# Moving the convolution norms of the last eight token tiles out of the attention-only stage

## The reference

```python
# convolution y from an FFT of the S4D taps, then:
r = x + (y + x * D)
out = (r - mean(r)) * rsqrt(var(r) + 1e-5) * ln_w + ln_b     # norm 0
x = layernorm(x + out)                                       # norm 1
x = layernorm(x + cross_attention(x, ctx))                   # norm 2
x = layernorm(x + mlp(x) + experts(x))                       # norm 3
# experts: top-8 of 64 keys on each of two sides, 4 heads; top-8 of the 64 sums;
# softmax over them; silu(x . down[idx]) * weight, times up[idx], summed
```

## Time and profile before

| | us |
|---|---|
| median of 3 runs | 667.06 |
| lowest, highest | 664.38, 668.99 |
| the profiled execution, its own time | 664.58 |
| its span | 662.8 |

### The profile page before, as it was taken

How to read it: one execution, slowest core, us unless ns; L and a number is a source line. 1 busy time by engine, 2 the same in 40 slices (tenths; PEclk the granted TensorE clock), 3 DMA queues, 4 the chain that set the end, 5 groups by cost and what they waited for, 6 DMA issues and landing times.

```text
span 662.8 us, 9603 instructions
## 1 busy us (share of the span) xinstructions
PE 580.7 (88%) x3132; PEld 376.8 (57%) x3132; DVE 491.4 (74%) x966; ACT 397.5 (60%) x554; POOL 310.4 (47%) x346
## 2 busy tenths in 40 slices
PE   5568688937695989999999999998999999998996
PEld 2246465726363644547775654776655588443585
DVE  7997966483468868978568797857779795778782
ACT  4776463311432659976548786673878773777760
POOL 0747576592524474433536342364632352753451
PEclk9679999977957689999999999999999999999999
DMA  8591325684610000000000000000000000000000
GB/s 233 195 389 41 104 74 154 165 209 28 257 60 0 2 0 0 1 0 1 1 0 17 8 10 1 0 1 0 17 9 8 0 1 1 17 8 8 0 15 18
DMA packets 19851, 34.13 MB, mean 51 GB/s; under 512 B 7265, under 2 KB 14178, under 8 KB 18338
## 3 DMA queue, kind: packets, MB, share of 16 engines
q1 hardware_dynamic: 15425, 29.32, 14.4%
q10 hardware_dynamic: 4376, 4.20, 2.1%
HBM read 21.81 MB, written 10.52 MB: 49 GB/s over the span
## 4 chain that ended last, share of the span: by engine, by line
PE 68%; DVE 13%; ACT 9%; issue 5%; POOL 3%; DMA 2%; POOLq 0%; DVEq 0%; ACTq 0%; SPq 0%
PE banks L820 22%; PE banks L910 8%; PE banks L915 8%; PE banks L865 5%; PE banks L887 3%; PE banks L842 3%; PE banks L877 3%; PE banks L708 3%; PE banks L698 2%; PE banks L735 2%; PE banks L851 2%; ACT arena L931 2%; DVE stats L1460 2%; PE banks L902 2%; DVE arena L1548 1%
## 5 line engine op out<-in xcount | busy, mean ns | idle before, releaser
L1256 POOL TENSOR_TENSOR arena<-arena 128x1024 f32<-128x1024 f32 x64 | 126.3, 1973 | 156.2 <-ACT arena L1129 155.1
L820 PE MATMUL banks<-arena 128*128 128x512 f32 x384 | 174.2, 596 | 6.0 <-issue 3.9
L820 PEld LDWEIGHTS banks<-arena 128*128 128x128 f32 x384 | 69.9, 190 | 83.4 <-issue 77.5
L1129 ACT ACTIVATE arena<-arena 128x1024 f32<-128x1024 f32 x64 | 73.5, 1149 | 7.5 <-DVE arena L1546 3.2
L1131 ACT ACTIVATE arena<-arena 128x1024 f32<-128x1024 f32 x64 | 73.5, 1149 | 2.1
L1548 DVE SCALAR_TENSOR_TENSOR arena<-arena 128x1024 f32<-128x1024 f32 x48 | 65.1, 1357 | 1.7
L1227 POOL TENSOR_SCALAR arena<-mv 128x1 f32<-128x1 f32 (+1 forms) x40 | 14.4, 360 | 104.0 <-DVE mv L1461 102.6
L1019 ACT COPY arena<-banks 128x512 f32<-128x512 f32 (+1 forms) x64 | 34.1, 532 | 46.8 <-PE banks L812 31.2
L910 PE MATMUL banks<-arena 128*128 128x256 f32 x256 | 58.4, 381 | 2.7 <-DVE arena L1570 1.3
L915 PE MATMUL banks<-arena 128*128 128x256 f32 x256 | 57.9, 379 | 0.0
L1033 ACT ACTIVATE tok<-tok,arena,rstd 128x256 f32<-128x256 f32 x48 | 27.9, 598 | 44.9 <-POOL arena L1232 44.0
(11 more groups left out here) (181 smaller groups left out, 1065.9 us busy)
## 6 DMA issues: line engine op xcount, KB each, us to landing
scr_x<-arena SPq DMA_DIRECT2D x16, 256.0 KB, 2.6
arena<-scr_x SPq DMA_DIRECT2D x2, 2048.0 KB, 11.2
scr_z<-arena ACTq DMA_DIRECT2D x14, 256.0 KB, 4.4
tok<-in_x SPq DMA_DIRECT2D x8, 256.0 KB, 5.8
arena<-scr_z SPq DMA_DIRECT2D x4, 512.0 KB
out<-tok SPq DMA_DIRECT2D x16, 128.0 KB, 1.7
arena<-scr_z SPq DMA_DIRECT2D x2, 640.0 KB
arena<-in_imat SPq DMA_DIRECT2D x1, 1152.0 KB, 5.5
```

Source lines behind the costliest of these rows:

```text
L820: ins = mm(bk[:, :], w[:, k, P * m:P * m + P], src[:, k, :], start=(k == 0), stop=(k == KC - 1))
L1129: fn(ebuf[m % 2], sxb[m % 2], ACT.Prelu, bias=negt[:, n % 2, h:h + 1], alpha=FAR).then_inc(s_ranked, 1)
L1256: tt(sxb[m % 2], sim[:, n % 2, h, 0:XR].unsqueeze(2).broadcast_to((P, XR, NKEYS)), sim[:, n % 2, FH + h, :].unsqueeze(1).broadcast_to((P, ...
```

## The change

The places of the five steps after `conv` are no longer the same pattern for all pairs. Pairs 0 to 3 keep theirs. Pairs 4 to 7 take theirs from a table. Pair 4 moves from places 1.60 to 2.30 to 2.0 to 2.55, pair 5 from 2.03 to 2.73 to 3.0 to 3.5, pairs 6 and 7 from 2.69 to 3.50 to 7.2 to 8.1. That late, `hid` would have overwritten their rows, so the two have room of their own beyond it. No instruction is added or taken away, no shape changes, and the `conv` steps stay.

```diff
-         "ln": (-1.672, -1.4042, 0.3146, 1.2224, 1.9378, 2.3695, 3.0308, 3.1386),
+         "ln": (-1.672, -1.4042, 0.3146, 1.2224),
...
+NORM_LATE = {4: (2.0, 2.05, 2.35, 2.2, 2.55), 5: (3.0, 3.05, 3.3, 3.15, 3.5),
+             6: (7.46, 7.2, 7.375, 7.42, 7.6), 7: (7.9, 7.65, 7.87, 7.9, 8.1)}
...
         for k, kind in enumerate(("ln", "dev0", "residual", "dev1", "norm1")):
-            steps.append((PLACE["ln"][q] + PLACE["ln_steps"][k], (kind, q)))
+            steps.append((NORM_LATE[q][k] if q in NORM_LATE else PLACE["ln"][q] + PLACE["ln_steps"][k], (kind, q)))
...
-        rconv = part("rconv", o_w + 4096, TILES, D)
+        rconv_of = [part(f"rconv{h}", at, B, D) for h, at in enumerate(
+            [o_w + 4096 + B * D * q for q in range(NQ - 2)] + [o_ext, o_ext + B * D])]
...
-                    nc.scalar.copy(rconv[:, 2 * n:2 * n + 2, :].rearrange("p a b -> p (a b)"), src).then_inc(s_wact, 1)
+                    nc.scalar.copy(rconv_of[n].rearrange("p a b -> p (a b)"), src).then_inc(s_wact, 1)
...
-                        statistics(0, 2 * n + b, rconv[:, 2 * n + b, :], b == 1)
+                        statistics(0, 2 * n + b, rconv_of[n][:, b, :], b == 1)
```

More of the change, by code:

```diff
@@ L1483, in _ @@
                     for b in range(B):
-                        link(stt(gtmp[:, b, :], rconv[:, 2 * n + b, :], mv[:, 0, 2 * n + b, 0:1], lnw,
+                        link(stt(gtmp[:, b, :], rconv_of[n][:, b, :], mv[:, 0, 2 * n + b, 0:1], lnw,
                                  ALU.subtract, ALU.mult))
```

## The result

The changed kernel takes 673.95 us in the median of 5 runs (673.21 to 676.26), the kernel before 667.06 in 5 runs beside it (664.38 to 671.64): a ratio of 1.011, 95% interval 1.0057 to 1.0162. It is slower by about 1%, 6.9 us in the median and 9.3 between the two profiled spans (672.1 against 662.8). The forecast was 670, the range 663.5 to 674.5: the time lies inside, near the upper end.

What follows compares the result with a forecast made beforehand. The prediction took the DVE, POOL and ACT chain to bound the fill and PE the outer products. Its terms, -4.5 + 4.1 + 2.9 + 0.7 = +3.2 us, gave 667.8 against the profiled 664.58, or 670 as median; range 663.5 to 674.5.

Steps and rivals of the forecast that it cites:

- the forecast itself: Whole kernel: the main case, a change of +1 to +6 us, given a chance of 0.62.
- Term 1: Fill: the DVE, POOL and ACT chain shortens and PE's long `attend` wait goes; 4.5 us gained, bounds 2.6 and 7.4.
- Term 2: `outer` 1: DVE idles 5.9 us for `dev0` 6 behind the last `sums`, so PE stands; 4.1 us lost.
- Term 3: `outer` 2: `ln` 7 and `residual` 7 lengthen DVE's work, so PE waits for `spread` (2, 1); 2.9 us lost.
- Term 4: ACT: `norm1` 7 enters its dense run behind the second feed-forward's first product; 0.7 us lost.
- The clock pays for it: Fill: less PE idle time keeps the granted clock up; gain 7.4 us, sum +0.3, 667 us median; chance 0.19.
- DVE becomes the bound past `outer` 2: From 320 to 350 us DVE has no idle time, delaying tile 3's `spread`; sum 7 to 9 us; chance 0.14.
- They hide it all: Outer products: DVE's idle time absorbs the new work, leaving the fill's gain, 660 to 663 us median; chance 0.05.
- The Trainium skill's rule on shared interfaces: Outer products: GpSimd contends with two-input DVE operations, stretching residuals and `sums`; the sum some 1 us worse.

Runs made afterwards that it cites:

- e6: The changed kernel with the first half of `outer` 1 computed twice, filling PE's first wait; 673.0 us, 1.0074 of the kernel before.
- e11: The changed kernel with both PE waits filled, by 16 and 8 needless matmuls in `outer` 1 and 2; 672.88 us, 1.0061 of before.
- e7: e3 with tile 3's last two `sums` narrowed to 16 elements a partition, leaving out part of its scores; 663.42 us, 0.9922 of before.
- e9: The changed kernel with the residuals of pairs 6 and 7 moved behind the outer products; 667.38 us, 0.9966 of before.
- e12: e9 with residual 6 in DVE's idle time ahead of `project` 7 and pair 7's statistics behind `outer` 3; 664.6 us, 0.994 of before.
- e3: The changed kernel with `dev0` 6 placed ahead of the last two `sums` of tile 3 on POOL; 671.7 us, 1.0078 of before.
- e4: The changed kernel with pair 6's statistics and `dev0` before the last `sums`, residual 7 behind `total` 3; 667.46 us, 0.9976 of before.
- e13: e9 with residual 6 also among the second feed-forward's inner products, near residual 7; 670.74 us, 1.0021 of before.
- e2: The changed kernel with only pairs 6 and 7 moved, pairs 4 and 5 at their old places; 673.58 us, 1.0093 of before.
- e8: The changed kernel with places spread out: residual 6 earlier, residual 7 in the second feed-forward, pairs 4 and 5 later; 672.42 us, 1.0063 of before.
- e10: e9 with pairs 4 and 5 back at their places before the change; 666.92 us, 0.9972 of before.

## Why the prediction was right in its mechanism and short in its size

| term | forecast | measured between the profiles |
|---|---|---|
| 1, fill | -4.5 | -4.4 at `score` (4, 0), -4.3 at `project` 3, then -2.3 at `outer` 0 |
| 2, `outer` 1 | +4.1 | wait 4.04, then 6.40 for 3.62: in all +7.0 |
| 3, `outer` 2 | +2.9 | wait 1.98: in all +2.3 |
| 4, ACT | +0.7 | wait 0.57, then 1.26 for 0.79 and 4.89 for 3.72: in all +2.4 |
| sum | +3.2 | +9.3 |

"In all" is taken from the starts of PE's steps, so that the rows add up. The median moved by 6.9, the profiles by 9.3. The time fell into the range partly by luck: +6.9 is more than the +1 to +6 of the forecast itself (its chance was 0.62) and than the 1% that it took for no difference, and the range reaches that far only because it pairs the lowest gain with a loss of 8.8 and adds a little for a rival that did not come.

**Term 1** came step by step. The second part of `attend` 2 was to start at 210.8; all 20 of its matmuls now run without a wait from 210.33 on, the ninth at 211.9. DVE was to idle 2.6 us ahead of each residual and did 2.8; the score of 219.42 was to be at 215.2 and was at 215.57. Up to `project` 3 the gain is 4.3. Then the clock was at 0.57 from 229 to 241 us, `sim` took 3.78 for 1.98 and the four transposes behind it 1.06 for 0.66: 2.0 us given back. The prediction had this as its lower bound, one query more at the low level, 2.6; it was a `sim`.

**Term 2** failed in no step of DVE or POOL: 6.02 us of DVE idle time for 5.9 forecast, 4.04 for 4.1. What failed is the sentence "That is 4.1 us in which PE stands": the price of a wait of PE was taken as its length. Behind it PE ran at 1.2 GHz and took 2.78 us more. e6 shows the cause, since it fills the wait and the slow matmuls are gone, and e11 its size: with both waits filled the late loss is 7.7 us, against 11.65 in the change. These 7.7 are 4.3 + 2.6 + 0.8, next to the 4.1 + 2.9 + 0.7 of the forecast; the remaining 4.0 us are the clock's.

**Term 3** took DVE for dense from `score` (8, 0) to the end of `spread` (2, 1), 16.3 us. It was 18.3 (327.76 to 346.10), since DVE still idled 1.51 us for PE's slow second half of `outer` 1 and 1.06 for `attend` 7. PE was late itself by then, so its own wait was 1.98 and not 2.9; with the clock up, in e11, term 3 is 2.6. **Term 4** is `norm1` 7 in ACT's dense run, 0.8 in e11; the rest of its 2.4 is the low clock near 370 us.

**The rivals.** "The clock pays for it" looked at the clock on one side only, as something that the fill might win. The fill did win it in some traces, but from about 219 us on and not in the change: the fill is 6.0 to 6.1 us shorter in e6, e7, e9 and e12 and 2.5 to 2.9 in the change, e3, e4, e11 and e13, and all nine run the same instructions in the same order up to the sixth `expert` product. "DVE becomes the bound past `outer` 2" gives nearly the measured sum (+7 to +9), by another way: PE had no wait at tile 3's `spread`. "They hide it all" fell with the `sums` at 321.15. The Trainium skill's rule on shared interfaces (GPSIMD Engine Reference, Key points), which the prediction weighed at some 1 us, changed nothing in the change itself, where residual 6 starts after the last `sums` and takes 1.01; it decided e3.

**The loss was in the places, not in the move.** The 9.6 us of DVE work cost 1.6 us where they mostly fall into idle time (e12), 2.3 behind the outer products (e9), 5.1 close together there (e13), and 11.7 ahead of the `spread` steps that the outer products wait for.

**What stays open.** Why the fill takes the one or the other course is not settled: the instructions are the same, and a profile shows one execution. The medians are mixtures: of e12's twelve runs, the five with a mean granted clock of 0.944 or more took 661.48 to 663.7 us, the seven with 0.937 or less 664.27 to 669.84. That is the likely reason why e9, with -3.7 us by its profile, an execution of 662.27 us, has a median only 1.2 us below before (its runs go from 660.95 to 672.71). Nor is it settled why the clock falls again near 370 us: in the change, e2, e3 and e6 it does, behind a wait of 0.57 us that in e7 and e11 had no such effect. In all four it had fallen at the outer products already, 25 to 39 us earlier; in e7 and e11 it had not, and e4, which fell there too, has no such wait and no second fall. That is a pattern in seven traces, not a tested cause.

## What to carry to other kernels

Price a wait of TensorE at its length plus what the clock takes behind it, and, as far as these traces go, prefer several waits of under 2 us to one long one; from 300 us on, all the falls but those near 370 us came behind waits of 2.1 us or more. Move work of another engine by the idle times of that engine that end with something nobody waits for, and count what it is longer than the idle time as its least cost: that came out in e12 (0.6 us) and was too little in e13, where two such pieces stood close together. Before placing a VectorE operation with two SBUF inputs, look what GpSimd does at that moment, and the other way round.

## What the runs showed of the hardware

- TensorE's granted clock after a wait, from 300 us on: at 0.5 behind waits of 4.04 us (the change), 4.03 (e2), 2.29 (e3), 2.28 (e6) and 2.10 (e4), still at 1.00 behind 2.11 (e13), 2.05 (e8), 1.99 (e2 and e7), 1.98 (the change), 1.72 (e3), 1.62 (e13), 1.53 (e9 and e10) and 1.08 (e12). The longer waits let it fall, the shorter ones did not, near 2.1 us both happened, and the fall near 370 us behind 0.57 came only in traces with an earlier one.
- The same instructions run the fill with and without a low stretch at about 230 to 241 us, a difference of 3 us of 670. The Trainium skill (TensorE: Matmul & The Clock Gate, Part 1) says that the number of slow matmuls at the start of one kernel varies from run to run; these traces, of nine kernels that are alike up to the sixth `expert` product, agree, and show it in the middle of the kernel too.
- DVE operations with two SBUF inputs beside POOL's 128x1024 addition: 2.69 us for 1.01 (two operations) and 2.01 for 0.48, while POOL's own took 1.90 and 2.10. It goes the other way too: an operation of POOL of 128x1, the first of a `dev2` or `dev3`, that takes 0.25 us at 221.67 in the change took 1.24 there at 332.64, and 1.08 to 1.18 in three places of the kernel before, each time beside a DVE operation with two SBUF inputs that had started first, and ended 0.08 or 0.09 us behind it. The change:

```profile
332.52 1.28 DVE L1551 SCALAR_TENSOR_TENSOR arena<-arena 128x1024 f32<-128x1024 f32 x1
332.64 1.24 POOL L1230 TENSOR_SCALAR arena<-mv 128x1 f32<-128x1 f32 x1 [5.01 <-DVE mv L1464]
```

  In these rows the engine that starts second waits nearly to the end of the other's operation.
